# Attention cores with 16-wide heads: the rows of negated maxima go ahead of the group loads in SyncE's queue

## The reference

```python
q = (query @ wq.T + bq).reshape(B, Sq, NUM_HEADS, D_K).transpose(0, 2, 1, 3)
k = (key @ wk.T + bk).reshape(B, Sk, NUM_HEADS, D_K).transpose(0, 2, 1, 3)
v = (value @ wv.T + bv).reshape(B, Sk, NUM_HEADS, D_K).transpose(0, 2, 1, 3)
scores = jnp.einsum('bhqd,bhkd->bhqk', q, k) / SCALE
attn = jax.nn.softmax(scores, axis=-1)
out = jnp.einsum('bhqk,bhkd->bhqd', attn, v)
```

## Time and profile before

| what | value |
|---|---|
| time, three runs | 4907.15, 4916.33, 4920.60 us; median 4916.33 |
| the profiled execution | 4910.83 us, of which the span is 4909.0 |
| TensorE busy | 4175.8 us, 85% of the span |
| VectorE, ScalarE, GpSimd busy | 2875.6, 2348.4, 1358.6 us |

### The profile page before, as it was taken

How to read it: one execution, slowest core, us unless ns; L and a number is a source line. 1 busy time by engine, 2 the same in 40 slices (tenths; PEclk the granted TensorE clock), 3 DMA queues, 4 the chain that set the end, 5 groups by cost and what they waited for, 6 DMA issues and landing times. The chain is left out here.

```text
span 4909.0 us, 69714 instructions
## 1 busy us (share of the span) xinstructions
PE 4175.8 (85%) x20384; PEld 1981.0 (40%) x20384; DVE 2875.6 (59%) x6517; ACT 2348.4 (48%) x4572; POOL 1358.6 (28%) x1202
## 2 busy tenths in 40 slices
PE   8779856689788997897979699999998988489986
PEld 6322445386552333573334233333335544222224
DVE  4558474401667884005861378787873256388866
ACT  4447331243244774333754355454552246269993
POOL 0122141211101111112110188787883212101112
PEclk9669988799887998897989799999999989689998
DMA  8545212354033332674335422111210034623421
GB/s 288 118 101 123 52 38 35 142 198 145 25 131 67 63 63 66 246 242 135 81 83 197 150 71 66 61 61 61 69 51 24 22 113 96 152 48 92 96 55 38
DMA packets 332041, 486.56 MB, mean 99 GB/s; under 512 B 84516, under 2 KB 232596, under 8 KB 317252
## 3 DMA queue, kind: packets, MB, share of 16 engines
q1 hardware_dynamic: 325008, 449.92, 32.2%
q0 software_dynamic: 6384, 32.61, 2.1%
q10 hardware_dynamic: 348, 0.44, 0.0%
HBM read 327.63 MB, written 143.92 MB: 96 GB/s over the span
## 5 line engine op out<-in xcount | busy, mean ns | idle before, releaser
L1356 POOL TENSOR_TENSOR lc_totals<-lc_totals,lc_weights 128x1024 f32<-128x1024 f32 (+1 forms) x320 | 623.0, 1947 | 165.9 <-DVE lc_totals L1305 134.8
L1265 ACT ACTIVATE lc_weights<-ps 128x1024 f32<-128x1024 f32 x384 | 393.2, 1024 | 447.1 <-PE ps L1182 436.8
L1286 DVE TENSOR_REDUCE lc_part_max<-ps 128x2 f32<-128x1024 f32 x384 | 466.1, 1214 | 206.4 <-PE ps L1162 204.0
L1182 PE MATMUL ps<-lc_q,lc_k 64*128 64x512 f32 x1536 | 398.1, 596 | 4.8 <-issue 4.8
L1192 PE MATMUL ps<-lc_weights,lc_v 128*64 128x512 f32 x1536 | 371.7, 605 | 0.0
L866 DVE TENSOR_REDUCE l1x_core_part_max<-ps 128x1 f32<-128x512 f32 x512 | 316.4, 681 | 55.4 <-PE ps L690 55.3
L862 DVE CUSTOM_DVE_ANT_0 l3x_core_unused<-ps,l3x_core_mask_q 128x512 f32<-128x512 f32 x512 | 330.6, 686 | 6.9 <-DVE l3x_core_row_max L870 4.9
L825 ACT ACTIVATE l3x_core_weights<-ps 128x512 f32<-128x512 f32 x512 | 327.6, 694 | 7.3 <-PE ps L758 7.0
L825 ACT ACTIVATE l1x_core_weights<-ps 128x512 f32<-128x512 f32 x512 | 266.1, 603 | 84.0 <-PE ps L758 83.8
L808 ACT ACTIVATE ps<-l3x_core_mask_k 128x512 f32<-128x512 f32 x384 | 270.7, 705 | 35.9 <-DMA l3x_core_mask_k<-in_mask_k 35.9
L690 PE MATMUL ps<-l3x_core_k,l3x_core_q 96*128 96x512 bf16 x512 | 214.2, 419 | 56.0 <-DVE l3x_core_part_max L862 40.8
(11 more groups left out here) (493 smaller groups left out, 8574.1 us busy)
## 6 DMA issues: line engine op xcount, KB each, us to landing
cf_w<-in_L1f_w SPq DMA_DIRECT2D x32, 1024.0 KB, 7.5
lc_k<-latent_k SPq DMA_DIRECT2D x32, 768.0 KB, 6.6
lc_v<-latent_values SPq DMA_DIRECT2D x32, 768.0 KB, 4.9
latent_k<-feed_staged SPq DMA_DIRECT2D x64, 256.0 KB, 2.6
latent_values<-feed_staged SPq DMA_DIRECT2D x64, 256.0 KB, 2.0
k_heads<-proj_parts SPq DMA_DIRECT2D x40, 384.0 KB, 2.6
q_heads<-proj_parts SPq DMA_DIRECT2D x32, 384.0 KB, 2.6
q_heads<-proj_parts SPq DMA_DIRECT2D x32, 256.0 KB, 3.0
```

The costliest lines, as they stand in the source:

```text
L1182: mm = nc.tensor.matmul(out[j], k_tile[g % RING][strip(j), i * P:(i + 1) * P], q_tile[g % RING][strip(j), :], start=False, stop=True)
L1265: nc.scalar.activation(weights[:, i % TILES, :, :], k.ps[:, B0 + (i % 2) * HEADS:B0 + (i % 2 + 1) * HEADS, 0:nq], ACT.Exp, scale=scale).th ...
L1286: nc.vector.reduce_max(own, k.ps[:, A0:A0 + HEADS, :], AX).then_inc(a_taken, 1)
L1356: nc.gpsimd.tensor_tensor(total, total, own, ALU.add).then_inc(added_by_pool, 1)
```

## The change

Only SyncE's order in `group(b, g)` of `attention_stage` is edited. Where the values are loaded by SyncE (`not kept`), the order becomes: wait for `pv_done`, values, row, loads of the stacks. Where they are not (`kept`), it becomes: row, wait for `pv_done`, loads of the stacks. No DMA is added or removed, no other engine's instructions change.

```diff
--- before.py
+++ after.py
@@ -639,14 +639,17 @@
 
             def group(b, g):
                 before = later(b, g, -1)
+                if exists(*before) and not kept:
+                    sync.wait_ge(pv_done, at(*before, nkt, nkt + ahead_tiles))
+                    if exists(*later(b, g, 1)):
+                        load_values(*later(b, g, 1))
+                if exists(*later(b, g, 1)):
+                    row(*later(b, g, 1))
                 if exists(*before):
-                    sync.wait_ge(pv_done, at(*before, nkt, nkt + ahead_tiles))
-                    if exists(*later(b, g, 1)) and not kept:
-                        load_values(*later(b, g, 1))
+                    if kept:
+                        sync.wait_ge(pv_done, at(*before, nkt, nkt + ahead_tiles))
                     if exists(*later(b, g, RING - 1)):
                         load_group(*later(b, g, RING - 1))
-                if exists(*later(b, g, 1)):
-                    row(*later(b, g, 1))
                 if by_batch and g == groups - 2 and exists(b + 1, 0):
                     sync.wait_ge(v_loaded[(groups - 1) % V_RING], v_done(b, groups - 1))
                     load_batch_values(b + 1)
```

## The result

The changed kernel takes 5009.55 us (median of 4 runs, 5000.98 to 5011.95), the kernel before 4915.63 us (median of 4 runs, 4907.15 to 4920.6). The ratio is 1.019, 95% interval 1.0171 to 1.0209: **slower, by 84 to 103 us**, inside the range and 26 us above the forecast of 4984.

A forecast was written before the change was run, and what follows sets the result against it. TensorE, busy 85% of 4909.0 us, was taken as the bound through its waits; later loads added 15.6, 7.8, 14.4 and 29.9 us in four short cores, 67.7 on 4910.83, giving 4984 on the median; range 4940 to 5030.

The forecast's parts named there:

- The mechanism: Four short attention cores: rows issue when made, loads start 3.45 us later, TensorE's gate of the next group waits for them.
- gates: First matmul of the maxima pass in each group (L690), which waits for the stacks loaded three groups ahead.
- the loads keep up: Rival for the whole kernel: loads land no later than their gate, waits for rows simply go, 4859 us; chance 0.08.
- made: Moment when GpSimd has the three parts of the row of negated maxima ready, before SP issues them.
- "Made" to gate: Short cores: rows 1.81 us, eight loads' issue 3.75, landing 2.8, 0.2 for registers and waking; 8.15 us, 8.60 in `l3a_core`.
- the landing: Last k load, issue to arrival: 2.8 us taken, the least seen; the median of 3.3 would add 24 us.
- SP's own time: Short cores: loads start 1.85 us behind "made", the last of eight is issued near 5.15, from one `pyr_coarse` passage.
- Gate to made in `pyr_core`: Maxima, transpose, negation and three GpSimd instructions: 4.78 us, giving steps of 12.93 us and +7.8 us for the core.
- the rival of the clock: TensorE's clock falls in 24 groups of `pyr_core` and `l2a_core`, 1.37 us each, +33 us: 5017 us; chance 0.22.
- Gate to made in `l3a_core`: 3.91 us at full clock, 5.28 at the lower clock taken from the second step on; +29.9 us for the core.

## Why the prediction was right, and where it was off

**The mechanism held** at each of its steps. Waits for rows are nearly gone (7.3 us left, all in `pyr_coarse`); there are 12 waits at the gates in each of four cores, each ended by the last of the loads; the rows go out as they are made and the loads behind them; `l1x_core` is unchanged:

```profile
1578.00:1948.00 370.00, 360.92 (x1991) 106.48 (x1994) 291.82 (x502) 274.31 (x527) 50.38 (x71) 0.99 0.27 53
```

(361.23 busy of 370 in the earlier trace rows); and the kernel with only the long cores changed confirms it. The rival "the loads keep up" would have needed them 6.8 us behind "made"; they came at 8.4 and more.

**The sum was 23 us short in the four cores.** Between the gates of groups 1 and 13 the forecast had +67.7; the gates of the changed kernel lie 158.8 us apart in `pyr_coarse` (152.6 forecast), 169.6 in `pyr_core` (155.2), 161.6 in `l2a_core` (155.2) and 160.9 in `l3a_core` (165.2), +90.5 in all. By terms:
- *"Made" to gate.* Forecast 8.15, measured in the mean of twelve steps 8.73 in `pyr_coarse`, 8.54 in `pyr_core` and 8.44 in `l2a_core`, and 8.59 in `l3a_core` where 8.60 was forecast. This is the term that was mis-sized, by (0.58 + 0.39 + 0.29) × 12 = 15 us. It was not the landing: the pick of 2.8 us in place of the median of 3.3 was right. In `pyr_coarse` the last load of a group landed 2.86 us after its issue began (mean of twelve), and before, with the row DMAs behind it, 3.75; the view of the tile `pyr_coarse_k`, where the earlier trace rows had 2.8/3.3/6.4, now has

```profile
DMA to landing us min/median/max: 2.4/3.1/4.6
```

  What was too small is SP's own time, read off one passage: the loads start 2.0 to 2.2 us behind "made" in the mean of each core (1.85 forecast, which holds for the first groups, 1.84 to 1.86), and from the first load's issue to the last one's pass 3.5 to 3.7 us in the three cores with eight loads (3.3 forecast). In `l3a_core`, with nine, it is 3.9 (3.75 forecast), and the term came out only because from the last issue to the gate passed 2.6 us where 3.0 was taken. In the timeline of the changed kernel the q loads of the next group, and the row and q loads of a group inside the loop, are

```profile
169.02 2.98 SPq L566 DMA_DIRECT2D pyr_coarse_q<-q_coarse  x4
...
194.22 1.80 SPq L602 DMA_DIRECT2D pyr_coarse_q<-pyr_coarse_max_parts  x3
196.23 1.91 SPq L566 DMA_DIRECT2D pyr_coarse_q<-q_coarse  x4
```

  The first takes 2.98 us, where the earlier trace rows had 1.89; in the loop SP needs 0.21 us between the last row DMA and the first load, where the first passage had 0.05. Why some issues take longer is open. The kernel with the rows sent twice shows that this time is paid for nearly in full at the gate.
  The Trainium skill's fixed cost of about 2.0 us per DMA ("DMA: Bandwidth & Descriptors", "Anatomy of one DMA — SWDGE (gpsimd) path") is stated for DMAs that GpSimd issues. These are issued by SyncE, the least landing of the k loads here is 2.4 us, and with 2.0 in the sum the forecast would have been farther off.
- *Gate to made in `pyr_core`.* Forecast 4.78 throughout; seven steps had 4.8 to 5.0, the other five 6.1 to 7.3: +10 us. In `l2a_core` one of twelve had 6.5, and the rest 4.8 to 5.0: +3. This was the rival of the clock, come true in 6 of 24 groups.
- *Gate to made in `l3a_core`.* Forecast 5.28 from the second step on; measured 4.0 to 5.6, in the mean 4.9: −4 us. In `pyr_coarse` 4.56 where 4.65 was taken: −1.

15 + 10 + 3 − 4 − 1 = 23.

**Some 11 us lie outside the four windows of steps.** The span grew by 100.9, the twelve steps of the table by 89.5. About 2 us are ahead of group 2 of `pyr_coarse`, 3 between `pyr_coarse` and `pyr_core`, 4 between `pyr_core` and `l2a_core`, 2 behind `l3a_core`. The kernel with the change in the `pyr` cores alone has the changed kernel's code in the first two of these stretches, and took 151.7 us up to "made" of group 2 (before 152.2, changed 154.1) and 69.8 us between the two cores (69.8 and 72.6): these 5 us are scatter between executions. The stretch between `pyr_core` and `l2a_core`, from "made" of group 14 to "made" of group 2, took 1843.0 us before, 1847.3 in the changed kernel, and 1844.3, 1845.5 and 1846.1 in the three kernels with the change in a part of the cores; `l1x_core`, which lies in it, took 279.3 us for twelve steps in all five. So the 11 us are of the size of that scatter, and I leave open whether some of them belong to the change.

In sum: the direction came from the landing computed against its reader, and that held, as did the choice of the landing time. The size was low because SP's own time was read off one fast passage and because the clock of `pyr_core` was taken at its cheaper end. Some of it is luck: the "made" to gate of `l3a_core` is right by two errors that cancel, the clock of `l3a_core` was taken too low by 4 us the other way, and the executions that were profiled lie 7 us farther apart than the medians. The measured 5009.55 is nearer to the rival with the clock lost everywhere (5017) than to my 4984, but that is chance: the clock fell in 6 of its 24 groups and cost 13 us there, not 33.

## What to carry to other kernels

Before a request is moved ahead of others in one issuing queue, count from the event that it waits for: all that it passes now starts behind that wait and behind the moved request's own issue (here 3.45 us, on loads with 1 us of slack, although the profile showed no wait for them). Where two kinds of requests stand in each other's way, none of the orders tried beat the one before; asking for one of them on an earlier event gave 22 us, and another engine's queue shortened the steps only in `pyr_coarse`, where ScalarE is busy for less than half of the time (63 of 138 us; in `l2a_core` 106 of 141). A time of issue read off one passage is a lower end: take the mean over the groups, in the loop too.

## What the runs showed of the hardware

Two stretches of `pyr_core` in the changed kernel, 7 us each, begin at the gates of groups 3 and 4; the columns are those of the windows above:

```profile
410.50:417.50 7.00, 7.00 (x21) 1.98 (x22) 3.93 (x7) 3.33 (x6) 0.90 (x3) 0.52 0.09 27
426.00:433.00 7.00, 7.00 (x39) 2.42 (x40) 6.14 (x12) 5.14 (x11) 1.22 (x3) 1.00 0.52 101
```

TensorE is busy all the time in both. In the first, ahead of which it had been idle 1.85 us, it got through 21 matmuls at a granted clock of 0.52, 1.2 GHz nearly throughout; in the second, after 0.65 us, through 39 at 1.00, 2.4 GHz. I had expected the fall only near an idle time of 1.7 us, and in `pyr_core` that is how it went: after 1.74, 1.85, 1.89, 2.04 and 2.59 us the step was slow, after 1.62 or less it was not. In `l2a_core`, with the same shapes, it was not: idle times of 1.96 and 1.99 us cost nothing and one of 1.63 did. So the idle time right ahead does not decide alone, and I have not found what does.

Three row DMAs (1x16x128 of bf16, 4 KB) hold the engine that issues them for 1.8 us, SP or ScalarE alike, 0.6 us each, and four loads (16x2048 or 48x2048 of bf16, 64 or 192 KB) mostly hold SP for 1.8 to 2.0 us, about 0.5 each: the issue of a small DMA is not cheaper than that of a large one here.

Alone on the queue, behind the rows, the last load of a group in `pyr_coarse` landed 2.5 to 3.1 us after its issue began, 2.86 in the mean of twelve. In the kernel before, with the row DMAs issued right behind it, it took 2.9 to 6.2 us, 3.75 in the mean, and was in by 0.7 us or more before the gate all the same.
